# Attention layers: the layer norm moves into the projection stage, tile by tile

## What is computed

```python
def _layernorm(x, axis=-1, eps=1e-05):
    m = jnp.mean(x, axis=axis, keepdims=True)
    v = jnp.var(x, axis=axis, keepdims=True)
    return (x - m) / jnp.sqrt(v + eps)
...
        q = rope(proj(wq, bq))
        k = rope(proj(wk, bk))
        v = proj(wv, bv)
```

## Time and profile before

| | us |
|---|---|
| median of three runs | 5742.93 (5742.36 to 5756.35) |
| the profiled execution | 5715.51, of which span 5713.8 |
| busy: PE, DVE, ACT, POOL | 4713.6, 3783.7, 3163.8, 1683.8 |
| mean granted TensorE clock | 0.923 of 2.4 GHz |

### The profile page before, as it was taken

One profiled execution on the slowest core, in us unless ns is written; L12 is line 12 of the kernel. 1 busy time (PEld: TensorE's weight loads), 2 busy tenths in 40 slices (PEclk: granted clock), 3 DMA queues, 4 the chain that ended last, 5 costly groups with the idle time before them and its releaser, 6 DMA issues. The chain is left out here.

```text
span 5713.8 us, 91311 instructions
## 1 busy us (share of the span) xinstructions
PE 4713.6 (82%) x33501; PEld 2077.9 (36%) x33596; DVE 3783.7 (66%) x4596; ACT 3163.8 (55%) x6002; POOL 1683.8 (29%) x1468
## 2 busy tenths in 40 slices
PE   5677668998579977799778998589867799799999
PEld 2233223443233336333353333256422344333344
DVE  6899658886589943899448882677539710799400
ACT  5656444766448853488535885444466422488621
POOL 0666315886032215322252220000006400222100
PEclk7899888999789989899898998799989999799999
DMA  0000001111021125211242110000000000111100
GB/s 28 0 1 1 4 28 55 44 45 29 10 72 50 49 74 168 74 49 51 91 150 71 48 52 15 2 10 2 4 10 0 21 0 0 40 38 38 43 0 15
DMA packets 120296, 211.54 MB, mean 37 GB/s; under 512 B 34982, under 2 KB 71442, under 8 KB 118484
## 3 DMA queue, kind: packets, MB, share of 16 engines
q1 hardware_dynamic: 110580, 182.00, 10.4%
q10 hardware_dynamic: 4320, 15.73, 0.9%
q0 software_dynamic: 4992, 8.41, 0.5%
HBM read 153.93 MB, written 52.00 MB: 36 GB/s over the span
## 5 line engine op out<-in xcount | busy, mean ns | idle before, releaser
L958 ACT ACTIVATE l_core_probs<-l_core_ps_scores_b 128x512 f32<-128x512 f32 (+3 forms) x3840 | 1610.1, 508 | 584.6 <-PE l_core_ps_scores_b L866 419.4
L1060 DVE TENSOR_REDUCE l_core_chunk_max<-l_core_ps_scores_a 128x2 f32<-128x1024 f32 (+3 forms) x1280 | 1253.2, 1020 | 84.3 <-PE l_core_ps_scores_a L851 48.9
L866 PE MATMUL l_core_ps_scores_b<-l_q_rows_sb,l_k_rows_sb 64*128 64x512 bf16 (+3 forms) x3840 | 948.7, 333 | 39.9 <-ACT l_core_probs L958 16.6
L851 PE MATMUL l_core_ps_scores_a<-l_k_rows_sb,l_q_rows_sb 64*128 64x512 bf16 (+3 forms) x3840 | 741.2, 345 | 104.0 <-DVE l_core_chunk_max L1060 44.9
L1009 POOL TENSOR_SCALAR_AFFINE_SELECT l_core_probs<-l_core_probs 128x512 f32<-128x512 f32 x512 | 325.8, 636 | 1174.4 <-ACT l_core_probs L958 1169.7
L881 PE MATMUL l_core_ps_acc<-l_core_probs,l_v 128*9 128x512 f32 (+3 forms) x6144 | 648.8, 494 | 15.9 <-ACT l_core_out_sums L932 8.6
L866 PEld LDWEIGHTS l_core_ps_scores_b<-l_q_rows_sb,l_k_rows_sb 64*128 64x128 bf16 x3840 | 304.4, 94 | 702.4 <-ACT l_core_probs L958 614.1
L1060 DVE TENSOR_REDUCE l_core_neg_max<-l_core_ps_scores_a 128x2 f32<-128x256 f32 (+3 forms) x640 | 493.3, 819 | 95.7 <-PE l_core_ps_scores_a L811 93.5
L1931 POOL TENSOR_TENSOR l_scan_bx<-l_xs,l_scan_b_rows 128x1024 f32<-128x1024 f32 x192 | 452.3, 2356 | 224.2 <-DVE l_scan_states L1941 217.9
L1941 DVE TENSOR_TENSOR_SCAN l_scan_states<-l_scan_ps_decay,l_scan_bx 128x1024 f32<-128x1024 f32 x192 | 439.7, 2290 | 40.8 <-POOL l_scan_bx L1931 15.3
L979 POOL TENSOR_TENSOR l_core_probs_decayed<-l_core_probs,l_decay 128x1536 f32<-128x1536 f32 (+2 forms) x160 | 394.0, 2487 | 145.9 <-ACT l_core_probs L958 145.9
(11 more groups left out here) (323 smaller groups left out, 7761.4 us busy)
## 6 DMA issues: line engine op xcount, KB each, us to landing
l_slots_weights<-m_both_dram SPq DMA_DIRECT2D x78, 512.0 KB, 4.6
l_q_rows_sb<-l_q_rows SPq DMA_DIRECT2D x128, 96.0 KB
l_k_rows_sb<-l_k_rows SPq DMA_DIRECT2D x128, 96.0 KB
l_heads_out<-l_core_out_sums SPq DMA_DIRECT2D x300, 32.0 KB
l_q_rows<-l_proj_parts SPq DMA_DIRECT2D x36, 256.0 KB
l_k_rows<-l_proj_parts SPq DMA_DIRECT2D x36, 256.0 KB
l_q_rows_sb<-l_q_rows SPq DMA_DIRECT2D x128, 64.0 KB
l_k_rows_sb<-l_k_rows SPq DMA_DIRECT2D x128, 64.0 KB
```

The source lines that it names most:

```text
L851: mm = nc.tensor.matmul(slot[:, i, 0:w], qs[n % 3][rows, p, qt * P:(qt + 1) * P], ks[n % 3][rows, p, c * NT:c * NT + w], start=True, stop= ...
L866: mm = nc.tensor.matmul(pb[m % 3][:, 0:w], ks[n % 3][rows, p, kt * P:(kt + 1) * P], qs[n % 3][rows, p, q0:q0 + w], start=True, stop=not diag)
L958: nc.scalar.activation(pt[:, ts % RP, j, 0:w], pb[m % 3][:, 0:w], ACT.Exp, scale=scale).then_inc(b_free, 1)
L1060: nc.vector.tensor_reduce(to, pa[e % 2][:, :, 0:width_a(qt, c)], AX.X, ALU.max, negate=True).then_inc(a_free, 1)
```

## The change

The call of `layer_norm` goes, with its stage and barrier, and its operations move into the blocks of `attn_project`. PE's loop now runs over steps t = 0 to 10: centering t, variance t-1, and the products of tile t-3. The buffers of the norm have two places each instead of four, so that centering t waits for the normalising of tile t-2, and wv's products use the banks of `centered`. DVE's step t evicts both halves of tile t-4 ahead of normalising tile t-1; in plain layers third n-5 stands behind value n. ACT's step t is the square of tile t, the logarithm and exponential of tile t-1, then for the two values n = 2t-10 and 2t-9 the first part of n and the second part of n-1. Plain values have eight places (`t1`, and `t2` for odd batches); rope values keep the four of `t1`, with `t2` as scratch. The loops over tiles on PE, DVE and POOL are written out. The loads of weights are issued at the head of SP's block.

```diff
--- before.py
+++ after.py
@@ -480,7 +480,7 @@
 def attn_project(net, tag, w, dq, rope, bias, decay, parts, v, qs, ks, load_stack, load_consts_):
 
 
-    nc, xn, dram = net.nc, net.xn, net.dram
+    nc, x, xn, dram = net.nc, net.x, net.xn, net.dram
...
-        layer_norm(net, tag + "_ln", loads=loads)
         part = sb("parts", [P, 2, 3, T], BF16)
         pq = ps("qk", [P, 4, NT])
-        pv = ps("v", [P, 2, NT])
+        cen = ps("centered", [P, 2, NT])
+        var = ps("var", [P, 2, NT])
+        pv = cen
+        sq, lnv, rstd = (sb(n, [P, 2, NT]) for n in ("squares", "log_var", "rstd"))
+        cen_ready, sq_ready, var_ready, ln_ready, rstd_ready, xn_ready, loaded = (sem(n) for n in (
+            "centered", "squares", "var", "log_var", "rstd", "xn", "loaded"))
         mm_ready, mm_free, v_ready, v_free = (sem(n) for n in ("mm", "mm_free", "v_mm", "v_free"))
         val, hi, rest, mid, low, made, stored, t_free = (sem(n) for n in (
             "value", "hi", "rest", "mid", "low", "made", "stored", "t_free"))
         first_stored, rows_clear = sem("first_batch_stored"), sem("rows_clear")
         NW = len(ws)
+
+        def value(b, m):
+            return (t2 if b % 2 and not rope else t1)[0:R, m % 2, m // 2, :]
...
+                for to, source in loads:
+                    sp.dma_start(to, source).then_inc(loaded, 16)
                 sp.wait_ge(rows_clear, 6)
                 load_consts_(sp)
...
-                with pe.Fori(0, TILES) as i:
+                def center(t):
+                    if t >= 2:
+                        pe.wait_ge(xn_ready, t - 1)
+                    nc.tensor.matmul(cen[:, t % 2, :], net.center[:, :], x[:, t * NT:(t + 1) * NT],
+                                     start=True, stop=True).then_inc(cen_ready, 1)
+
+                def variance(t):
+                    pe.wait_ge(sq_ready, t + 1)
+                    if t >= 2:
+                        pe.wait_ge(ln_ready, t - 1)
+                    nc.tensor.matmul(var[:, t % 2, :], net.mean[:, :], sq[:, t % 2, :],
+                                     start=True, stop=True).then_inc(var_ready, 1)
+
+                def project(i):
+                    pe.wait_ge(xn_ready, i + 1)
+                    if i == 0:
+                        pe.wait_ge(loaded, 16 * len(loads))
                     for j in range(2):
                         pe.wait_ge(mm_free, 2 * i + j + 1)
                         for m in range(j, NW, 2):
-                            mm = nc.tensor.matmul(pq[:, m, :], ws[m][:, :], xn[:, ds(i * NT, NT)],
+                            mm = nc.tensor.matmul(pq[:, m, :], ws[m][:, :], xn[:, i * NT:(i + 1) * NT],
                                                   start=True, stop=True)
                         mm.then_inc(mm_ready, 1)
+
+                for t in range(TILES + 3):
+                    if t < TILES:
+                        center(t)
+                    if 1 <= t <= TILES:
+                        variance(t - 1)
+                    if t >= 3:
+                        project(t - 3)
...
-                    if n >= 4:
-                        dve.wait_ge(low, n - 3)
+                    if n >= 8:
+                        dve.wait_ge(low, n - 7)
...
+                        nc.vector.tensor_copy(value(n // 4, n % 4), pq[0:R, j, :]).then_inc(val, 1)
...
-                if rope:
-                    with dve.Fori(0, B) as b:
...
-                    for n in range(4 * B):
-                        plain_value(n)
-                        if n >= 3:
-                            plain_third(n - 3)
-                    for n in range(4 * B - 3, 4 * B):
+                def turned(n):
+                    h, j = n // 2 % 2, n % 2
+                    dve.wait_ge(mm_ready, n + 1)
+                    dve.wait_ge(t_free, n + 1)
...
+                def norm(t):
+                    dve.wait_ge(rstd_ready, t + 1)
+                    nc.vector.tensor_tensor(xn[:, t * NT:(t + 1) * NT], cen[:, t % 2, :], rstd[:, t % 2, :],
+                                            ALU.mult).then_inc(xn_ready, 1)
+
+                for t in range(1, TILES + 4):
+                    if t == 4:
+                        dve.wait_ge(loaded, 16 * len(loads))
+                    if t >= 4:
+                        for n in (2 * t - 8, 2 * t - 7):
+                            if rope:
+                                turned(n)
+                                continue
+                            plain_value(n)
+                            if n >= 5:
+                                plain_third(n - 5)
+                    if t <= TILES:
+                        norm(t - 1)
+                if not rope:
+                    for n in range(4 * B - 5, 4 * B):
                         plain_third(n)
...
-                for b in range(B):
-                    for m in range(4):
-                        first(b, m)
-                        if m:
-                            second(b, m - 1)
-                    second(b, 3)
+                nc.scalar.preload_act_table_set("natural_log_exp_and_others")
+
+                def square(t):
+                    act.wait_ge(cen_ready, t + 1)
+                    if t >= 2:
+                        act.wait_ge(var_ready, t - 1)
+                    nc.scalar.activation(sq[:, t % 2, :], cen[:, t % 2, :], ACT.Square).then_inc(sq_ready, 1)
+
+                def root(t):
+                    act.wait_ge(var_ready, t + 1)
+                    if t >= 2:
+                        act.wait_ge(rstd_ready, t - 1)
+                    nc.scalar.activation(lnv[:, t % 2, :], var[:, t % 2, :], ACT.Ln, bias=net.ln_eps).then_inc(ln_ready, 1)
+                    act.wait_ge(ln_ready, t + 1)
+                    if t >= 2:
+                        act.wait_ge(xn_ready, t - 1)
+                    nc.scalar.activation(rstd[:, t % 2, :], lnv[:, t % 2, :], ACT.Exp, scale=-0.5).then_inc(rstd_ready, 1)
+
+                for t in range(TILES + 5):
+                    if t < TILES:
+                        square(t)
+                    if 1 <= t <= TILES:
+                        root(t - 1)
+                    if t >= 5:
+                        for n in (2 * t - 10, 2 * t - 9):
+                            first(n // 4, n % 4)
+                            if n:
+                                second((n - 1) // 4, (n - 1) % 4)
+                second(B - 1, 3)
...
-                with pool.Fori(0, B) as b:
+                for b in range(B):
```

More of the change, by code:

```diff
@@ L574, in plain_third @@
                     dve.wait_ge(mid, n + 1)
-                    nc.vector.tensor_tensor(part[0:R, j, 2, tok], t1[0:R, j, h, :], part[0:R, j, 1, tok],
+                    nc.vector.tensor_tensor(part[0:R, j, 2, tok], value(n // 4, n % 4), part[0:R, j, 1, tok],
                                             ALU.subtract).then_inc(low, 1)
-                if rope:
-                    with dve.Fori(0, B) as b:
[L580 to L595, removed]
-                    for n in range(4 * B):
-                        plain_value(n)
-                        if n >= 3:
-                            plain_third(n - 3)
-                    for n in range(4 * B - 3, 4 * B):
@@ new lines, in turned @@
+                def turned(n):
+                    h, j = n // 2 % 2, n % 2
+                    dve.wait_ge(mm_ready, n + 1)
+                    dve.wait_ge(t_free, n + 1)
+                    nc.vector.scalar_tensor_tensor(t1[0:R, j, h, :], pq[0:R, j, :], bcol[0:R, j:j + 1],
+                                                   tab[0:R, 0, h * NT:(h + 1) * NT], ALU.add, ALU.mult)
+                    nc.vector.scalar_tensor_tensor(t2[0:R, j, h, :], pq[0:R, 2 + j, :], bcol[0:R, 2 + j:3 + j],
+                                                   tab[0:R, 1, h * NT:(h + 1) * NT], ALU.add, ALU.mult
+                                                   ).then_inc(made, 1)
+                    dve.wait_ge(made, n + 1)
+                    nc.vector.tensor_tensor(t1[0:R, j, h, :], t1[0:R, j, h, :], t2[0:R, j, h, :],
+                                            ALU.add).then_inc(val, 1)
+                    dve.wait_ge(val, n + 1)
+                    dve.sem_inc(mm_free, 1)
@@ L620, in first @@
                     act.wait_ge(val, 4 * b + m + 1)
-                    nc.scalar.activation(part[0:R, j, 0, ds(b * S + h * NT, NT)], t1[0:R, j, h, :],
+                    nc.scalar.activation(part[0:R, j, 0, ds(b * S + h * NT, NT)], value(b, m),
                                          ACT.Copy).then_inc(hi, 1)
@@ L626, in second @@
                     act.wait_ge(rest, 4 * b + m + 1)
-                    nc.scalar.activation(part[0:R, j, 1, ds(b * S + h * NT, NT)], t1[0:R, j, h, :],
+                    nc.scalar.activation(part[0:R, j, 1, ds(b * S + h * NT, NT)], value(b, m),
                                          ACT.Copy).then_inc(mid, 1)
-                for b in range(B):
-                    for m in range(4):
-                        first(b, m)
```

(11 more changed lines are left out.)

3 lines of the change are left out of this document (1 added, 2 removed).

## The result

The changed kernel takes 5759.62 us in the median of 16 runs (5749.42 to 5765.15), the kernel before 5742.43 us in as many (5733.18 to 5756.35). The medians differ by 17.2 us, or 0.30%, against +24.8 us in the prediction; the ratio on record, which is not the quotient of the two medians, is 1.0025 with an interval of 1.0017 to 1.0033. So the kernel is slower, by an amount just at the 0.3% that the prediction took as its bound of the measurable.

A forecast was written before the change was run, and what follows sets the result against it. No engine is full; chains and whatever ends last bound the merged stages. Terms -1.3 + 8.2 + 11.9 + 6.0 = +24.8 us gave a forecast of 5768 us (+0.43%), with half to double clock term 5759 to 5786, whole range 5742 to 5793.

The forecast's parts named there:

- the rope loop: Rope layers: from value 5 to 9 each odd value waits for the odd one before, 10.7, 10.1 and 9.9 us.
- rival (c): Rope layers: ACT's second parts come early enough, value 3's lead of 9.3 us lasts; -20 us, 5723; chance 0.10.
- the second store: Plain layers: SP's stores of values 4 to 7; the stage ends 25.7 us after they start (26.9 in layer 14).
- the ring: Rope layers: the wait of value 2t-7 on `t_free`, through POOL, ACT, PE and DVE; 10.7 us a tile.
- plain layers, full clock: Three plain layers at 2.4 GHz: third 7 is 0.8, 0.4 and 0.1 us ahead in layers 2, 8, 14; -1.3 us.
- rope layers, full clock: Layers 4 and 6 at 2.4 GHz: value 9 at 56.5 against 53.2, each layer 4.1 us late; +8.2 us.
- clock in norm turns: Norm-only turns at 1.2 GHz: two slow turns in layers 2 and 4, one in the other three; +11.9 us.
- clock in rope loops: Rope steps t = 7 and 8 slowed by PE's lower clock: half of 6.0 us a layer, +6.0 in both.
- the plain tail: Layer 8, from tile 7 normalised at 35.3 us to third part 7, taken at 42.4 us.
- (a): Rival: PE's clock stays at 2.4 GHz throughout; sum +6.9 us, 5750; chance 0.15.
- (b): Rival: PE's clock falls in all norm turns and rope loops; +51 us, 5794; chance 0.13.
- (d): Rival: parts miss by their errors, or plain tail 2 to 3 us a layer earlier; 5743 +- 10; chance 0.12.

The follow-up runs named there:

- The two ways of opening the ring: Changed kernel with ACT's four copies first in rope layers, 5690.84 us (ratio 0.9967); or with eight places for rope values, 5696.4 us (0.9975).
- the kernel with rope layers apart: Changed kernel with the merged stage in plain layers only, rope layers keeping norm and projection of before: 5705.43 us in one run, beside 5712.02 before.

## Why the prediction was right, and which sizes were off

**What decides.** Right: the rope loop closes, rival (c) fails, and the plain layers end a nearly fixed time behind the second store (25.9 to 27.7 us in all variants). The two ways of opening the ring and the kernel with rope layers apart show the first two; the stores of every run show the last.

**How near the edge.** The forecast's own range, with half to double the clock term, began at 5759, and the measured median is 5759.62. It is there by luck in part: the clock, for which that range was made, came out at its full size, and what is missing is 8.6 us in the plain layers, an error that the range did not allow for.

**The sum, term by term.** I take the clock out by the two runs with extra products (10.1 + 6.5 us), supposing that the two add, which was not run together. Each measured term is a difference of single stages, good to about 1 us a layer, and the slow pair of products in layer 6, which neither run removed, is left in the second row.

| term | predicted | measured |
|---|---|---|
| plain layers, full clock | -1.3 | -4.0 -2.7 -3.2 = -9.9 |
| rope layers, full clock | +8.2 | 18.4 - 1.8 - 6.5 = +10.1 |
| clock in norm turns | +11.9 | 10.1 |
| clock in rope loops | +6.0 | 6.5 |
| sum | +24.8 | +16.8 |

**The term that was mis-sized** is the plain tail: tile 7 to third part 7. I had tile 7 at 35.3 in layer 8, and with the clock held up it is there at 35.3, by two errors that cancel: tile 4 came 1.4 us later, at 23.3, and ACT's turn was 4.0 us in place of 4.45. But behind it I put three pairs of 1.7 us and two third parts at the 1.50 us that one had taken beside POOL. Layer 8 after, timeline of DVE and POOL behind tile 7:

```profile
3048.75 0.68 DVE L629 TENSOR_TENSOR x_norm<-l_proj_ps_centered,l_proj_rstd 128x512 f32<-128x512 f32 x1
3049.22 8.99 POOL L716 TENSOR_TENSOR l_proj_t<-l_proj_t,l_proj_parts 128x512 f32<-128x512 f32 x6 [0.94 <-ACT l_proj_parts L667]
3049.35 0.73 DVE L598 TENSOR_SCALAR l_proj_t<-l_proj_ps_qk,l_proj_bias_cols 128x512 f32<-128x512 f32 x1
3050.23 0.69 DVE L609 TENSOR_TENSOR l_proj_parts<-l_proj_t,l_proj_parts 128x512 bf16<-128x512 f32 x1
...
3053.30 0.75 DVE L609 TENSOR_TENSOR l_proj_parts<-l_proj_t,l_proj_parts 128x512 bf16<-128x512 f32 x1
```

Third parts 5 to 7 took 0.69 to 0.75 us and a pair 1.55: third 7 is made 4.6 us behind tile 7, where I had 7.1. By the trace POOL was at work all the while. Its six subtractions took 1.50 us each, where one alone takes 1.15, so here POOL had the longer instructions and not DVE. In the kernel before, too, only one third part in four took 1.49 to 1.50 us in layer 8 (those of values 2, 6 and 10, to value 11) and the others 0.69; I had priced two of three by the slow one. With the clock up the second stores are at 40.4, 40.0 and 39.3, 2.4 us or more ahead of mine. So with the clock up the merge pays about 3 us in each plain layer, and the clock takes most of it back.

**The rope term.** Value 3 came at 27.2, not 25.8, since slow norm turns delay it (24.9 with the extra products there). The loops of 11.4, 10.5 and 12.5 stand against 10.7, 10.1 and 9.9; the last is 10.2 with the clock held up, so its terms were sound. The first is not long by the clock: PE's instructions between value 3 and value 5 that the loop crosses ran at 2.4 GHz (1.02 us a centering or variance), and with all of them and the next products fast, in layer 6 with extra products, it still took 11.3. Its excess lies in two terms that POOL and DVE have beside each other: the subtraction took 1.51 us in place of 1.15 and the eviction of value 5 2.8 in place of 2.3.

**The clock.** I took 17.9 us between bounds of 0 and 44; the two runs give 16.6. That the two nearly agree says little of how I split the term, since a slow turn moved from one place to another between executions. The rule of the Trainium skill (TensorE: Matmul & The Clock Gate, "A second HAM failure mode: psum-queue depth-cycling") agrees with the trace in kind: PE swings between the two levels as it pauses for its buffers. A term near the upper bound, which I drew from it, does not: once products fill the pauses, normalisings are 3.7 to 4.2 us apart and stay so.

**Rivals.** (a), a clock at 2.4 GHz throughout, would by the same runs have given about 0 and not +6.9. (b) is out by its size; its 5794 also lay just outside the 5793 that the prediction gave as the end of its whole range. (d) is half true: its condition on the plain tail was met, third 7 came 2.5 us earlier a layer than I had it, but this did not cancel the ring and the clock, and the measured time is 7 us above its edge of 5753.

## What to carry to other kernels

When two stages are merged into one, follow a buffer's release through every in-order queue it crosses: if a step on engine A for an old tile stands behind a step for a new tile that itself waits for the buffer, the pipeline becomes a ring, and its pace is the sum of its members (10 to 12 us here), not the slowest engine (6 us). The signature is several engines idle in the same stretch, each for another of them, while none is full. Put the old tile's steps ahead of the new one's in each engine's program before buying buffers: the order alone was worth 18 us a rope layer, four further places 12.5. Where eight places already keep the ring open, as in the plain layers, the copies ahead made no difference; whether the order would open it there with four places was not run.

## What was not expected of the hardware

Work that nothing uses made the stages shorter: two products of 0.85 us in each of two pauses saved up to 3.7 us a layer, and eight in a rope ring 2.6 and 3.9. They do not remove every slow turn: in layer 6 the slow pair of products (3.60 us behind a pause of 3.07) only moved to a place where it counted. When DVE and POOL work side by side, either can have the longer instruction: in layer 8 one third part in four took 1.50 us on DVE in the kernel before, and none of thirds 5 to 7 in the kernel after, while POOL's subtractions took 1.50 in place of 1.15. What decides this was not tested.
